# A decoder layer on one core: the cross attention rewritten tile by tile, with a narrower top-32 search, marks that GpSimd multiplies in, and heads added on TensorE

## The reference

```python
Q = (x_text @ Wq).reshape(Bb, Tt, H, DH)          # H = 4 heads of DH = 32
K = (x_vision @ Wk).reshape(Bb, Gg, H, DH)        # Gg = 2048 keys
scores = jnp.einsum('bthd,bghd->bhtg', Q, K) / np.sqrt(DH)
scores = jnp.where(vision_mask[:, None, None, :], scores, -jnp.inf)
topv, topi = jax.lax.top_k(scores, K_TOP)         # K_TOP = 32
probs = jax.nn.softmax(topv, axis=-1)
attn = jnp.zeros_like(scores).at[bi, hi, ti, topi].set(probs)
attn_mean = attn.mean(axis=1)
V = x_vision @ Wv
c_t = jnp.einsum('btg,bgd->btd', attn_mean, V)
```

## Time and profile before

| | |
|---|---|
| three runs | 5827.6, 5832.1 and 5834.4 us, median 5832.1 |
| span of the profiled execution | 5836.0 us |
| busy over the whole span | PE 68%, PEld 52%, DVE 56%, POOL 35%, ACT 27% |
| stage_cross | 1814.7 us |

### The profile page before, as it was taken

The page is one execution under the profiler, slowest core; times in us unless marked ns, Lnnn a source line. Parts: engine busy times, 40 slices in busy tenths (PEclk is TensorE's granted clock), DMA queues, the critical chain, the costliest instruction groups (busy, mean ns, idle before and its releaser), DMA issues. The chain is left out here.

```text
span 5836.0 us, 62332 instructions
## 1 busy us (share of the span) xinstructions
PE 3947.5 (68%) x17990; PEld 3006.7 (52%) x18052; DVE 3252.9 (56%) x9545; ACT 1604.9 (27%) x2170; POOL 2014.8 (35%) x1374
## 2 busy tenths in 40 slices
PE   2422159996355455444545698796789999499998
PEld 1321037774233333233323486575668888388887
DVE  8959914442888888888888254552234343422222
ACT  1211013333555555444555100002221111111111
POOL 2447100000333433333433265140147676233332
PEclk8555569998666666666666799898889999799999
DMA  0025032225101001001100144223322121200000
GB/s 11 15 77 204 29 83 71 80 78 174 44 8 48 21 10 48 19 7 39 29 10 6 68 141 141 87 94 132 117 85 82 58 75 51 90 19 22 23 23 20
DMA packets 243466, 356.11 MB, mean 61 GB/s; under 512 B 67844, under 2 KB 121988, under 8 KB 238856
## 3 DMA queue, kind: packets, MB, share of 16 engines
q1 hardware_dynamic: 137728, 175.01, 10.1%
q10 hardware_dynamic: 102920, 169.93, 8.5%
q0 software_dynamic: 2560, 8.39, 0.4%
HBM read 246.29 MB, written 106.96 MB: 61 GB/s over the span
## 5 line engine op out<-in xcount | busy, mean ns | idle before, releaser
L2764 DVE CAST m_act_hl<-m_g 128x512 fp32r<-128x512 f32 x256 | 138.1, 539 | 894.9 <-ACT m_g L2652 894.9
L1381 POOL TENSOR_TENSOR xa_acc<-xa_acc,xa_prob 128x2048 f32<-128x2048 f32 x96 | 437.8, 4560 | 515.9 <-ACT xa_prob L1483 515.9
L2513 POOL TENSOR_TENSOR m_act_hl<-m_g,m_act_hl 128x512 fp32r<-128x512 f32 x256 | 353.3, 1380 | 702.6 <-DVE m_act_hl L2764 702.6
L1581 DVE MAX8 xa_cand<-xa_s_buf 128x8 f32<-128x64 f32 x4096 | 531.7, 210 | 52.2 <-issue 52.0
L2652 ACT ACTIVATE m_g<-m_ps_h,m_b 128x512 f32<-128x512 f32 x256 | 176.5, 689 | 1103.2 <-PE m_ps_h L82 1103.2
L1402 PE MATMUL xa_ps_f<-xa_ones,xa_flag 128*1 128x1 f32 x256 | 24.2, 164 | 629.5 <-DVEq L1597 629.3
L80 PE MATMUL m_ps_h<-m_hT,m_w 128*128 128x512 f32 x1024 | 412.7, 403 | 12.3 <-DVE m_w L2743 7.6
L1395 PE MATMUL xa_ps_s<-xa_ks,xa_qs 128*128 128x512 f32 x512 | 372.1, 810 | 70.4 <-ACT xa_s_buf L1476 36.4
L81 PE MATMUL m_ps_h<-m_hT,m_w 128*128 128x512 f32 x1024 | 404.8, 395 | 0.0
L82 PE MATMUL m_ps_h<-m_hT,m_w 128*128 128x512 f32 x1024 | 404.5, 395 | 0.0
L82 PE MATMUL m_ps_o<-m_w,m_act_hl 128*128 128x512 f32 x1024 | 404.3, 395 | 0.0
(11 more groups left out here) (374 smaller groups left out, 9957.3 us busy)
## 6 DMA issues: line engine op xcount, KB each, us to landing
at_xk<-in_x_dram SPq DMA_DIRECT2D x128, 128.0 KB, 2.7
xa_ks<-kt SPq DMA_DIRECT2D x64, 256.0 KB, 4.8
spectrum<-df_yo ACTq DMA_DIRECT2D x32, 512.0 KB, 2.8
id_raw<-spectrum SPq DMA_DIRECT2D x32, 512.0 KB, 3.8
m_xt<-x ACTq DMA_DIRECT2D x64, 256.0 KB, 3.3
bf_w_dn<-_L_ffn_down_weights_dram SPq DMA_DIRECT2D x7, 2048.0 KB, 7.2
bf_w_up<-in_L_ffn_up_weights_dram ACTq DMA_DIRECT2D x7, 2048.0 KB, 10.4
ky_raw<-in_ctx_dram SPq DMA_DIRECT2D x16, 768.0 KB, 6.6
```

Of the source, the lines that this page charges most:

```text
L1381: pool.tensor_tensor(acc[:, k, :], acc[:, k, :], prob[:, h % 2, :], ALU.add).then_inc(s_acc, 1)
L1581: dve.max(out=cand[:, 8 * g:8 * g + 8], in_=s_buf[:, slot, g * SEG:(g + 1) * SEG])
L2513: pool.tensor_tensor(lo, g32[:, :], hi.bitcast(F32), ALU.subtract).then_inc(s_gl, 1)
```

## The change

Work is arranged by tile of four heads, and all loops are unrolled over the 32 tiles.

- **Search.** DVE still finds the 8 largest of each segment, but writes them by rank. The 32 largest are looked for among 104: the three largest of each segment (96) and the 8 largest of all the rest (a MAX8 over 160). The flag counts the eighth of these 8, and the eighth of each segment. Flags of all four heads are summed by one matmul, read by four loads and settled together, after 16 of the 32 searches of the next tile's first head.
- **Select.** DVE writes for each head a mark of 0 or 1 in bf16 (keep), after the flags are settled. ACT computes the exponentials in place, and POOL multiplies the marks in, each head in two halves of 1024 columns.
- **Scale, turn and add.** DVE writes four diagonal matrices with the reciprocals. PE multiplies each 128 x 128 block of each head by its head's diagonal and adds the four heads in PSUM: 64 fp32 matmuls a tile in place of the 16 transposes. ACT's scaling and POOL's sums go.
- **Mask.** stage_keys writes the mask's rows once to DRAM as 0 or -1e30; SP loads them as a 97th row of the keys against a row of ones in the queries, and the bf16 matmuls go. For that POOL clears 32 partitions of the keys' and queries' tiles at the stage's start, and SP waits for it.

```diff
--- before.py
+++ after.py
+                sp.dma_start(mask_u8[:, :], A["mask_BxS2_bf1"].rearrange("(o b) s -> o (b s)", o=1)).then_inc(s_ms, 16)
+                sp.wait_ge(s_mask, 1)
+                sp.dma_start(km_out.rearrange("(o b) s -> o (b s)", o=1), mask[:, :].bitcast(F32)).then_inc(s_mst, 16)
...
+                dve.wait_ge(s_ms, 16)
+                dve.tensor_scalar(mask[:, :], mask_u8[:, :], BIG, -BIG, ALU.mult, ALU.add).then_inc(s_mask, 1)
...
+    KEEP = 3
+    NW = 8 + KEEP * SEGS
+    NC = 8 + 8 * SEGS
+    BACK = NC - NW
+    HALF = S2 // 2
...
+                pool.memset(ks[96:128, :, :].bitcast(F32), 0.0)
+                pool.memset(qs[96:128, :, :, :].bitcast(F32), 1.0)
+                pool.drain().then_inc(s_const, 1)
...
+                def select(t, half, h):
+                    pool.wait_ge(s_exp, HEADS * t + h + 1)
+                    part = s_buf[:, t % 2, h, half * HALF:(half + 1) * HALF]
+                    pool.tensor_tensor(part, part, keep[:, h, half * HALF:(half + 1) * HALF], ALU.mult).then_inc(s_prod, 1)
...
+                for t in range(TILES):
+                    for h in range(HEADS):
+                        select(t, 0, h)
+                    if t % TPB == 0:
+                        context_lo(t // TPB, 0)
+                        context_lo(t // TPB, 1)
+                    select(t, 1, 0)
+                    select(t, 1, 1)
+                    lo(t, 0)
+                    lo(t, 1)
+                    select(t, 1, 2)
+                    select(t, 1, 3)
+                    if t % TPB == 0:
+                        context_lo(t // TPB, 2)
+                        context_lo(t // TPB, 3)
+                    lo(t, 2)
+                    lo(t, 3)
...
-                        pe.matmul(ps_s[:, c, :], qs[:, k, h, :], ks[:, h, c * 512:(c + 1) * 512], start=True, stop=False)
-                        last = pe.matmul(ps_s[:, c, :], row0[:, :], mask[:, c * 512:(c + 1) * 512], start=False, stop=True)
+                        last = pe.matmul(ps_s[:, c, :], qs[:, t % 2, h, :], ks[:, h, c * 512:(c + 1) * 512], start=True, stop=True)
...
+                def sum_flags(t):
+                    pe.wait_ge(s_cand, t + 1)
+                    if t >= 1:
+                        pe.wait_ge(s_chk, t)
+                    pe.matmul(ps_f[:, :], ones[:, :], flag[:, t % 2, :], start=True, stop=True).then_inc(s_f, 1)
+                def turn(t, half, h):
+                    pe.wait_ge(s_prod, 8 * t + 4 * half + h + 1)
+                    if h == 0:
+                        pe.wait_ge(s_diag, t + 1)
+                        if 4 * t + 2 * half >= 1:
+                            pe.wait_ge(s_a32, 4 * t + 2 * half)
+                    for c in range(8):
+                        k0 = half * HALF + c * P
+                        last = pe.matmul(ps_t[:, c // 4, c % 4, :], s_buf[:, t % 2, h, k0:k0 + P], diag[:, h, :],
+                                         start=(h == 0 and c % 4 == 0), stop=(h == HEADS - 1), skip_group_check=True)
+                    last.then_inc(s_dg, 1)
...
+                for t in range(TILES):
+                    sum_flags(t)
+                    if t >= 1:
+                        mix(t - 1)
+                    if t + 1 < TILES:
+                        scores(t + 1, 2)
+                    turn(t, 0, 0)
+                    turn(t, 0, 1)
+                    if t + 1 < TILES:
+                        scores(t + 1, 3)
+                    turn(t, 0, 2)
+                    turn(t, 0, 3)
+                    turn(t, 1, 0)
+                    if t + 2 < TILES:
+                        scores(t + 2, 0)
+                    turn(t, 1, 1)
+                    turn(t, 1, 2)
+                    turn(t, 1, 3)
+                    if t + 2 < TILES:
+                        scores(t + 2, 1)
+                mix(TILES - 1)
...
-                def scale(n, t, k, h, fresh):
-                    act.wait_ge(s_sel, n + 1)
-                    if h == 0 and not fresh:
-                        act.wait_ge(s_aT, 4 * (t - 1))
-                    act.activation(acc[:, k, :] if h == 0 else prob[:, h % 2, :], prob[:, h % 2, :], ACT.Identity,
-                                   scale=rec[:, h % 2, :]).then_inc(s_scl, 1)
...
+                def exponentials(t, h):
+                    act.wait_ge(s_keep, HEADS * t + h + 1)
+                    act.activation(s_buf[:, t % 2, h, :], s_buf[:, t % 2, h, :], ACT.Exp, bias=nmax[:, t % 2, h:h + 1],
+                                   scale=SCALE).then_inc(s_exp, 1)
...
+                for t in range(TILES):
+                    if t + 1 < TILES:
+                        copy(t + 1, 1)
+                    denominators(t)
+                    exponentials(t, 0)
+                    exponentials(t, 1)
+                    if t + 1 < TILES:
+                        copy(t + 1, 2)
+                    exponentials(t, 2)
+                    exponentials(t, 3)
+                    if t + 1 < TILES:
+                        copy(t + 1, 3)
+                    if t >= 1:
+                        mixed(t - 1)
+                    if t % TPB == 0:
+                        context_hi(t // TPB, 0)
+                        context_hi(t // TPB, 1)
+                    hi(t, 0)
+                    hi(t, 1)
+                    if t + 2 < TILES:
+                        copy(t + 2, 0)
+                    if t % TPB == 0:
+                        context_hi(t // TPB, 2)
+                        context_hi(t // TPB, 3)
+                    hi(t, 2)
+                    hi(t, 3)
...
+                ranks = cand[:, 8:NC].rearrange("p (r g) -> p r g", g=SEGS)
+                def scan(t, h, first, last):
+                    if first == 0:
+                        dve.wait_ge(s_sc, HEADS * t + h + 1)
+                    for g in range(first, last):
+                        dve.max(out=ranks[:, :, g], in_=s_buf[:, t % 2, h, g * SEG:(g + 1) * SEG])
+                def rank(t, h):
+                    k = t % 2
+                    dve.drain()
+                    dve.max(out=cand[:, 0:8], in_=cand[:, NW:NC])
+                    dve.drain()
+                    src = cand[:, 0:NW]
                     for r in range(TOPK // 8):
...
+                    dve.scalar_tensor_tensor(out=f_junk[:, :, :], in0=cand[:, :].rearrange("p (a x) -> p a x", a=2)[:, :, 0:NW],
+                                             scalar=top[:, k, h, TOPK - 1:TOPK], in1=f_weight[:, :, :],
+                                             op0=ALU.is_ge, op1=ALU.mult, accum_out=flag[:, k, h:h + 1])
+                    dve.drain()
...
+                def settle(t):
+                    k = t % 2
+                    if t >= 1:
+                        dve.wait_ge(s_prod, 8 * (t - 1) + 4 + 2)
+                    left = keep[:, 0:2, :].rearrange("p h s -> p (h s)").bitcast(F32)
+                    doubts = [dve.value_load(flag_i[0:1, h:h + 1], min_val=0, max_val=P * NW * 4) for h in range(HEADS)]
+                    for h in range(HEADS):
+                        with dve.If(doubts[h] > P * TOPK):
+                            src = s_buf[:, k, h, :]
...
+                def mark(t, h):
+                    if t >= 1:
+                        dve.wait_ge(s_prod, 8 * (t - 1) + 4 + h + 1)
+                    dve.tensor_scalar(keep[:, h, :], s_buf[:, t % 2, h, :], top[:, t % 2, h, TOPK - 1:TOPK], None,
+                                      ALU.is_ge).then_inc(s_keep, 1)
+                def diagonals(t):
+                    dve.wait_ge(s_den, HEADS * (t + 1))
+                    dve.reciprocal(rec[:, :], den[:, :])
+                    dve.drain()
+                    if t >= 1:
+                        dve.wait_ge(s_dg, 8 * t)
+                    for h in range(HEADS):
+                        dve.tensor_scalar(diag[:, h, :], ident[:, :], rec[:, h:h + 1], None, ALU.mult)
+                    dve.drain().then_inc(s_diag, 1)
...
-                def select(n, k, slot):
-                    dve.wait_ge(s_den, n + 1)
-                    dve.reciprocal(rec[:, k, :], den[:, k, :])
-                    dve.wait_ge(s_prob, n + 1)
-                    dve.scalar_tensor_tensor(out=prob[:, k, :], in0=s_buf[:, slot, :], scalar=top[:, k, TOPK - 1:TOPK],
-                                             in1=prob[:, k, :], op0=ALU.is_ge, op1=ALU.mult)
-                    dve.drain().then_inc(s_sel, 1)
...
+                for t in range(-1, TILES):
+                    more = t + 1 < TILES
+                    if more:
+                        scan(t + 1, 0, 0, 8)
+                    if t >= 0:
+                        dve.wait_ge(s_f, t + 1)
+                        dve.tensor_copy(flag_i[:, :], ps_f[:, :])
+                    if more:
+                        scan(t + 1, 0, 8, 16)
+                    if t >= 0:
+                        settle(t)
+                        for h in range(HEADS):
+                            mark(t, h)
+                        diagonals(t)
```

(8 more changed lines are left out.)

425 lines of the change are left out of this document (144 added, 281 removed).

## The result

The changed kernel takes 5651.9 us (median of 4 runs, 5645.3 to 5661.7) against 5833.2 us for the kernel before (4 runs, 5827.6 to 5835.3): a ratio of 0.969, 95% interval 0.968 to 0.971. That is 181 us less, where 73 were forecast. The direction was right and the time lies in the range of 5620 to 5890, though outside the narrower one of 5700 to 5830, and the gain is two and a half times as large as the forecast's.

A forecast was written before the change was run, and what follows sets the result against it. DVE's own row was taken as the bound; 41.1 us a tile plus GpSimd waits of 2.4, 2.1, 2.5 and 1.5 gave 49.6. With the ends, 73 us less than 5836, median 5760 us; own range 5700 to 5830, outer 5620 to 5890.

The forecast's parts named there:

- DVE's row, 41.1 us a tile: DVE's own instructions and settling for four heads, without GpSimd waits: 41.1 us, against 49.9 undisturbed and 52.8 measured before.
- Settling, 3.4 us (1.1 to 4.4): DVE reading four flags by loads, then four jumps: 3.4 us a tile, 1.1 if loads overlap wholly, 4.4 if nothing does.
- Mark 3 waits 2.4, the first diagonal 2.1: On DVE, GpSimd's first select delays the fourth mark 2.4 us and its second delays the first diagonal 2.1 us.
- the rival of dearer selects: GpSimd selects of 3.5 us, or PE staying at the low clock: tile of 53 to 56 us, 5870 to 5960 us; 13%.
- The third select at 15.1 to 16.6 us after the tile's flags' matmul, the mix ending at 10.2 to 11.7: GpSimd's third select waits for mix, scores, copy and exponential; mix ends at 10.2 to 11.7 us, the rest adds 4.9.
- About half of the tiles are caught, 2.5 us a tile: In about half the tiles one to three later DVE diagonals each wait for a GpSimd select: 2.5 us on average.
- The first rival: Loads and jumps cost 2.4 us or less, no tile's later diagonals are caught: 46.1 us a tile, 5650 us; 27%.
- C: The moment a tile's four flags are settled, when DVE's marks start; forecast at 5.85 us with a settling of 3.4.
- The flags' loss, 1.5 us: DVE's four flag instructions later in the tile now and then meet a GpSimd select or split: 1.5 us a tile.
- The ends: Outside the 31 periods: start 52.4 us, tail 65, three slow searches 68, splits at four batches 14, keys' stage 5 more.
- The rival on the other side: Settling of 4.4 us, each of three diagonals waits one select, 7.1 us instead of 2.5: 5893 us; 20%.
- The port rule: DVE's second port is shared, so GpSimd's instructions and DVE's two-port ones block each other; the skill names no price.

The follow-up runs named there:

- e6: Changed kernel with PE's scores of the next tile's head 2 ahead of the 48 matmuls of the mix: 5722.5 us, ratio 0.982.
- e7: Changed kernel with the four flags summed by four more PE matmuls, so DVE reads one load instead of four: 5594.0 us, ratio 0.960.
- e8: Changed kernel with e2, e3 and e7 joined, and scores computed over 97 partitions so the keys' tile needs no clearing: 5435.7 us, ratio 0.932.
- e5: e1 with the first head's ranking too put ahead of the settling: 5772.4 us, ratio 0.990.
- e9: Changed kernel with each GpSimd multiplication (select) cut from 1024 to 512 columns, 16 a tile: 5614.4 us, ratio 0.963.
- e11: e8 with the edit of e9 (selects of 512 columns): 5414.5 us, ratio 0.929.
- e10: e8 with the edit of e1 (settling behind all 32 searches): 5437.5 us, ratio 0.933.
- e12: e8 with the edits of both e9 and e1: 5413.8 us, ratio 0.929.
- e1: Changed kernel with flags settled, and marks and diagonals made, after all 32 searches of the next tile's first head instead of 16: 5634.0 us, ratio 0.966.
- e3: e2 with GpSimd's first select of a tile waiting until all four marks are written: 5482.5 us, ratio 0.941.
- e2: Changed kernel with the four diagonals made by ACT instead of DVE: 5546.3 us, ratio 0.951.

## Why the prediction was wrong, step by step

- **DVE's row, 41.1 us a tile.** Right in the sum. Ranking and flag of an undisturbed head take 3.49 us where 3.46 were forecast, a mark 1.28 where 1.2, a diagonal 0.27. The mean period of tiles without a slow search, the first left out, is 46.1 us; less the three waits below (1.9, 1.6 and 1.6) that leaves 41.0. It still holds 0.3 us that the prediction had no term for: the negated maxima too meet GpSimd (0.50 us in the mean, 0.17 alone).
- **Settling, 3.4 us (1.1 to 4.4).** Mis-sized: 2.8. The estimate of 0.7 a load was read from a single load with its jump. The loads start 0.61 us apart in the trace and the jumps 0.2, and the first load runs while searches are still queued. The 0.6 us did not shorten the row, since marks and diagonals together took as much more.
- **Mark 3 waits 2.4, the first diagonal 2.1.** Right in kind, 1.9 and 1.6 in size: a select takes 2.14 us, not the 2.36 taken from the earlier trace rows, and what is caught had to wait for the rest of one. The outer bounds of 1.3 and 4.5 us a select were both far off, so the rival of dearer selects did not come about.
- **The third select at 15.1 to 16.6 us after the tile's flags' matmul, the mix ending at 10.2 to 11.7.** Right: 15.9 and 10.9 in the tile shown. No row shows the bounds of 3.4 and 6.8 us for the clock's rise; in the trace of the kernel before it came 2.8 to 5.9 us after a mix's first matmul, in that of the changed kernel 3.3 to 6.1. The levels were as read from the earlier trace rows: three windows of the mix shown (columns as in the earlier trace rows) have 0.50, 0.67 over the rise, then 1.00.

```profile
2482.00:2484.00 2.00, 2.00 (x7) 2.00 (x7) 0.61 (x5) 0.00 (x0) 0.00 (x0) 0.50 0.00 0
2484.00:2486.00 2.00, 2.00 (x9) 2.00 (x9) 0.53 (x1) 0.59 (x4) 0.00 (x0) 0.67 0.02 4
2486.00:2488.00 2.00, 2.00 (x14) 2.00 (x13) 2.00 (x3) 1.94 (x7) 0.00 (x0) 1.00 0.00 0
```

- **About half of the tiles are caught, 2.5 us a tile.** This is the step that failed. It compared the third select with diagonals that were to run at 15.25 to 16.1 us. They ran at 13.9 to 14.7: 0.6 earlier for the settling, 0.75 for the two shorter waits. Both errors were small and within their bounds, but they had the same sign and stood before an on-or-off event: three of the 31 tiles were caught, 0 (nothing to mix yet), 18 and 22 (slow searches had given PE time to finish), and the last, in the tail. Instead of 49.6 the period was 46.1: of these 3.5 us 2.5 are this term, which came to nothing, and 1.0 the two waits that were forecast too long (3.5 in place of 4.5 together). 31 x 3.5 = 109 us is the error of 108, and of the 116 us by which the stage is shorter than its forecast (1620.9 against 1737). The first rival named this outcome, but its nearness, 2 us, is in part luck: it wanted a settling of 2.4 us or less, which took 2.8, and took C a microsecond earlier, which was 0.6; that the waits were a microsecond shorter, which it did not have, made up for a row that was a microsecond longer than its own. The prediction gave this case 27% and its own 40; with 3.5 us a tile between the two and a doubt of a microsecond on each side, nothing in the profile of before put one above the other.
- **The flags' loss, 1.5 us.** 1.6 measured in the sum, but e6, e7 and e8 show that it is no constant (0.7 to 2.5).
- **The ends.** First search 20.1 us after the stage's start (21.4 forecast), the first cast 32.2 later (31), 59.8 us from the last cast to the next stage (65); the two tiles with the three slow searches 72.9 us beyond the mean (68); the tiles at the start of a batch 49.4 to 49.9 us, 3.3 to 3.8 beyond it (3.5); the keys' stage 5.9 us longer (5).
- **The rival on the other side** exists as a mechanism: e5, with a settling that waits longer, is caught in 27 tiles at some 51 us a period, by two diagonals a tile that wait 1.9 us each, where the rival had three of 2.4. It would have needed 52.0 to be slower than before.
- **The port rule** of the Trainium skill (Advanced Engine Details and Errata, Mode Summary) holds here with the price that e9 puts on it: the rest of one GpSimd instruction a collision, but for the flag of 8.96 us in e11, which waited through four. The bf16 figure that the prediction set aside (VectorE: DVE Perf Modes, The perf-mode tier table, 0.69 us) was rightly left out: a mark with fp32 input and bf16 output takes 1.28 us.

What stays open: which pairs of the flags and selects collide is a matter of the phase between two queues; the flags' loss was measured in each kernel, but no run isolates it, so that part of the differences between e8, e10, e11 and e12 is read from the traces alone. That e1 came out 18 us faster was not expected by either theory and is not explained: its periods add up to what the changed kernel's do.

## What to carry to other kernels

Where two engines take turns, a wait hides in the duration of an instruction: compare the minimum and the mean of each line before trusting the table of waits. Group the instructions that can collide into a stretch in which the other engine is held back or has nothing to do, even by an added wait (e3, 64 us), or give them to a third engine (e2, 106 us); and cut the other engine's instructions short, since its length is the price; but short instructions catch more often, so that this alone gave 0.1 us a tile on marks and diagonals in e9, and paid on the flags once the others were out of the way (e11, 1.0 us a tile). When a forecast hangs on whether one event comes before another, and the margin is smaller than the error of the terms before it, say so and state two times: no mean of them will be measured.

## What was not expected of the hardware

- The edge is sharp: in one kernel and one execution, third selects at C+9.09 us or earlier made diagonals wait, and those at C+9.16 or later did not; the last diagonal starts at C+9.15.
- Data that is ready earlier can cost time: moving 4 matmuls ahead of 48 made the kernel 71 us slower (e6), and holding GpSimd back for 1.6 us a tile made it 64 us faster (e3).
- A load of a flag into a register and its bookkeeping take 0.61 us each when they follow one another, a jump 0.2, and a part of it hides behind queued searches (3.75 us idle behind a drain, 2.8 behind 8 searches, 2.2 behind 24).
- Of DVE's instructions, MAX8 and its replacement never lengthened beside GpSimd in the changed kernel (single searches 0.21 to 0.24 us, the replacements 0.25 to 0.26), nor did the reciprocal (0.16 to 0.17); tensor_scalar of 4, 128 and 2048 columns and the two-input flag did.
